# Three orders changed in a fused mixer and expert block: the second gate, the output's sum, and GpSimd's maps

## What is computed

```python
x = x + _layernorm(attn_ref(_layernorm(x)))
x = x + _layernorm(ffn_ref(_layernorm(x)))
```

```python
w = silu(einsum('btd,bthkd->bthk', h, de) * softmax(scores))
experts = einsum('bthk,bthkd->btd', w, ue)
```

## Time and profile before

| | |
|---|---|
| median of 3 runs | 2840.76 us (2839.64 to 2840.87) |
| profiled execution, its own time | 2840.37 us |
| its span, first to last instruction | 2838.7 us |
| TensorE matmuls busy | 2684.0 us, 95% |
| VectorE busy | 2449.3 us, 86% |
| GpSimd busy | 2100.9 us, 74% |
| ScalarE busy | 1737.2 us, 61% |
| mean granted clock of TensorE | 0.972 of full speed |

### The profile page before, as it was taken

The page is one execution under the profiler, slowest core; times in us unless marked ns, Lnnn a source line. Parts: engine busy times, 40 slices in busy tenths (PEclk is TensorE's granted clock), DMA queues, the critical chain, the costliest instruction groups (busy, mean ns, idle before and its releaser), DMA issues. The chain is left out here.

```text
span 2838.7 us, 50280 instructions
## 1 busy us (share of the span) xinstructions
PE 2684.0 (95%) x14720; PEld 2215.7 (78%) x14720; DVE 2449.3 (86%) x6310; ACT 1737.2 (61%) x3656; POOL 2100.9 (74%) x2689
## 2 busy tenths in 40 slices
PE   5899999999999999999999999999999999999985
PEld 4778887878887878887878887878887878887864
DVE  4588898998888998889898889988889988989985
ACT  4566666666666566666666666666666666666643
POOL 3377777877777877777877777877777877777866
PEclk9999999999999999999999999999999999999998
DMA  3000000000000000000000000000000000000000
GB/s 133 8 8 12 5 7 11 11 11 11 4 7 11 11 11 11 4 7 11 11 11 11 4 7 11 11 11 11 4 7 11 11 11 8 7 7 11 8 5 8
DMA packets 28182, 34.23 MB, mean 12 GB/s; under 512 B 2672, under 2 KB 27248, under 8 KB 27440
## 3 DMA queue, kind: packets, MB, share of 16 engines
q1 hardware_dynamic: 28144, 33.77, 3.8%
HBM read 25.37 MB, written 8.39 MB: 12 GB/s over the span
## 5 line engine op out<-in xcount | busy, mean ns | idle before, releaser
L1079 DVE SCALAR_TENSOR_TENSOR acc<-bank,cw,acc 128x253 f32<-128x253 f32 (+2 forms) x1920 | 773.5, 470 | 0.0
L1405 PE MATMUL bank<-hT,w_in 128*128 128x256 f32 x2560 | 606.3, 382 | 11.4 <-DVE acc L1079 10.8
L594 POOL TENSOR_TENSOR Em<-ee 128x1024 f32<-128x1024 f32 x256 | 578.8, 2280 | 11.3 <-issue 11.3
L1405 PEld LDWEIGHTS bank<-hT,w_in 128*128 128x128 f32 x2560 | 485.0, 192 | 118.2 <-issue 44.5
L1238 DVE SCALAR_TENSOR_TENSOR Em<-Em,p 128x1024 f32<-128x1024 f32 x256 | 407.1, 1590 | 0.0
L609 POOL TENSOR_TENSOR W<-W,Em 128x1024 f32<-128x1024 f32 x128 | 337.0, 2633 | 8.5 <-ACT Em L887 0.3
L755 ACT ACTIVATE acc<-bank,cb,cw 128x256 f32<-128x256 f32 x640 | 325.1, 561 | 0.0
L1247 DVE TENSOR_TENSOR Em<-Em,products 128x1024 f32<-128x1024 f32 x256 | 310.9, 1214 | 4.5
L887 ACT ACTIVATE Em<-Em,rden 128x1024 f32<-128x1024 f32 x256 | 292.0, 1142 | 33.9 <-DVE Em L1247 33.9
L1574 PE MATMUL products<-w_de,h2T 128*128 128x512 f32 x512 | 234.5, 601 | 17.7 <-DVE Em L1247 17.7
L736 ACT ACTIVATE xbcT<-acc 128x512 f32<-128x512 f32 x320 | 200.6, 627 | 74.1 <-DVE acc L1079 74.0
(11 more groups left out here) (196 smaller groups left out, 5578.9 us busy)
## 6 DMA issues: line engine op xcount, KB each, us to landing
x_in<-x_dram SPq DMA_DIRECT2D x32, 256.0 KB, 2.7
x_res<-x_dram SPq DMA_DIRECT2D x32, 256.0 KB, 2.7
out_dram<-f SPq DMA_DIRECT2D x32, 256.0 KB, 2.2
w_in<-in_wT_dram SPq DMA_DIRECT2D x1, 3080.0 KB, 12.0
w_up<-upT_dram SPq DMA_DIRECT2D x1, 1024.0 KB, 14.7
w_de<-down_eT_dram SPq DMA_DIRECT2D x1, 1024.0 KB, 16.7
w_down<-downT_dram SPq DMA_DIRECT2D x1, 1024.0 KB, 18.7
w_ue<-up_e_dram SPq DMA_DIRECT2D x1, 1024.0 KB, 20.8
```

Source lines behind the costliest of these rows:

```text
L594: nc.gpsimd.tensor_tensor(Em[:, k], bc(ee[:, k, 0:XD], 2, KEYS), bc(ee[:, k, XD:XD + KEYS], 1, XD), ALU.mult).then_inc(E_done.sem, 1)
L1079: ins = V.scalar_tensor_tensor(acc[:, r, a, ahead:], ps[:, a * TOK:(a + 1) * TOK - ahead], cw[:, t, k:k + 1], acc[:, r, a, ahead:], ALU.mu ...
L1405: last = mm(ring[j % 2][:, a * TOK:(a + 1) * TOK], w_in[:, k, at:at + P], hT[:, k, :], start=k == 0, stop=k == DK - 1)
```

## The change

- VectorE: the second gate and H's second step stand before the mask of head 2 of chunk 0, and `tail_sum` stands between the mask and the product of head 3.
- GpSimd: the second scaling of H stands before `ffn_root`; of chunk 1's maps only that of head 0 is formed ahead of `mixer_root_y`, and it waits for the second gate (`gate=g`); `tail_root3` follows `mixer_root_y`; the maps of heads 1, 2 and 3 stand in the next group's list, behind `tail_root4`, whose input the residual gives, and before the sums.
- ScalarE: silu of head 3's map stands in the next group's list, behind pairs 0 and 1; `ffn_norm` stands behind yT and the square of chunk 1.
- `clz` is multiplied with the divisor once for both chunks in `ffn_choose`; the product with the last expert goes into the silu as its scale, so that `ffn_last` is a copy only.
- TensorE: the product with zeros is left out; the first product of the accumulation marks the bank instead.

```diff
-            def weigh(e, c, *heads):
+            def weigh(e, c, *heads, gate=None):
+                if gate is not None:
+                    pool.wait_ge(y_done.sem, y_done.at(gate, CH - 1))
...
                 if c:
+                    weigh(f, 1, 1, 2, 3)
                     collect(f, 0, 2, 3)
...
                     mixer_scale(g, 1)
+                    mixer_decay(g, 1)
                 if c:
                     ffn_root(f)
-                if a:
-                    mixer_decay(g, 1)
-                if b:
-                    weigh(e, 1, 0, 1)
+                if b:
+                    weigh(e, 1, 0, gate=g)
                 if a:
                     mixer_root_y(g)
+                    tail_root3(g)
                 if b:
                     collect(e, 0, 1)
-                if a:
-                    tail_root3(g)
-                if b:
-                    weigh(e, 1, 2, 3)
...
-                    act.wait_ge(clz_done.sem, clz_done.at(e, c))
+                    act.wait_ge(clz_done.sem, clz_done.at(e))
+                    act.wait_ge(last_done.sem, last_done.at(e, c))
...
-                    nc.scalar.activation(cls[:], clz[:, c], ACT.Silu, accum_out=clsum[:, c:c + 1])\
+                    nc.scalar.activation(cls[:], clz[:, c], ACT.Silu, scale=last_a[:, 0:1],
+                                         accum_out=clsum[:, c:c + 1])\
...
                 pairs(0, 1)
+                if c:
+                    ffn_experts(f, 0, 3)
...
                     mixer_yT(g, 0)
-                if c:
-                    ffn_norm(f)
                 if b:
                     ffn_experts(e, 0, 1)
                 if a:
                     mixer_yT(g, 1)
                     mixer_square(g, 1)
+                if c:
+                    ffn_norm(f)
                 if b:
                     ffn_experts(e, 0, 2)
                     tail_keep(e)
-                    ffn_experts(e, 0, 3)
...
                 V.reciprocal(rden[:].rearrange("p c h -> p (c h)"), den[:]).then_inc(rden_done.sem, 1)
+                dve.wait_ge(rden_done.sem, rden_done.at(e))
+                dve.wait_ge(own_dve, own.n)
+                V.tensor_tensor(masked, masked, bc(rden[:].rearrange("p c h -> p (c h)"), 2, NC), ALU.mult)\
+                    .then_inc(clz_done.sem, 1)
...
-                dve.wait_ge(rden_done.sem, rden_done.at(e))
-                V.tensor_copy(last_a[:], fA[:, EXPERTS - 1:]).then_inc(own_dve, own.one())
-                dve.wait_ge(own_dve, own.n)
-                V.scalar_tensor_tensor(clz[:, c], clz[:, c], last_a[:, 0:1], bc(rden[:, c], 2, NC),
-                                       ALU.mult, ALU.mult).then_inc(clz_done.sem, 1)
+                if c or later(e):
+                    dve.wait_ge(cls_done.sem, cls_done.at(e, c - 1))
+                V.tensor_copy(last_a[:], fA[:, EXPERTS - 1:]).then_inc(last_done.sem, 1)
...
                     ffn_times(e, 0, 1)
-                    ffn_mask(e, 0, 2)
                 if a:
                     mixer_gate(g, 1)
                     mixer_step(g, 1)
                 if b:
+                    ffn_mask(e, 0, 2)
                     ffn_times(e, 0, 2)
                 if c:
                     ffn_store(f)
                 if b:
                     ffn_mask(e, 0, 3)
+                if a:
+                    tail_sum(g)
+                if b:
                     ffn_times(e, 0, 3)
-                if a:
-                    tail_sum(g)
...
-                    mm(f0[:], zero_b[:], mask_b[:].rearrange("p h t -> p (h t)"), start=True, stop=False)
                 for i in range(FT):
                     last = mm(f0[:, c * D:(c + 1) * D], hid[:, i, c * P:(c + 1) * P], w_down[:, i, :],
-                              start=False, stop=False)
+                              start=c == 0 and i == 0, stop=False)
```

More of the change, by code:

```diff
@@ L123, in sandwich @@
         ident_b = sb("ident_b", [P, P], BF16)
-        zero_b = sb("zero_b", [P, P], BF16)
         mask_b = sb("mask_b", [P, 4, P], BF16)
@@ L270, in sandwich @@
         Z_done = sig("Z_done", CH * RH)
-        clz_done, cls_done = sig("clz_done", CH), sig("cls_done", CH)
+        clz_done, last_done, cls_done = sig("clz_done"), sig("last_done", CH), sig("cls_done", CH)
         W_part, W_done = sig("W_part", CH * (RH - 1)), sig("W_done", CH)
@@ L341, in _ @@
             nc.gpsimd.memset(mask_b[:], 0.0).then_inc(own_pool, own.one())
-            nc.gpsimd.memset(zero_b[:], 0.0).then_inc(own_pool, own.one())
             nc.gpsimd.memset(halo[:], 0.0).then_inc(own_pool, own.one())
@@ L1325, in do_group @@
                     ffn_mask(e, 0, 3)
-                    ffn_times(e, 0, 3)
                 if a:
                     tail_sum(g)
+                if b:
+                    ffn_times(e, 0, 3)
                 dve.wait_ge(own_dve, own.n)
```

## The result

The changed kernel takes 2791.4 us (median of 4 runs, 2788.99 to 2792.48), the kernel before 2840.82 in the same comparison: a ratio of 0.9825, with an interval of 0.9808 to 0.9842. The forecast was 2746 with a range of 2718 to 2785. The gain is 49 us where 95 were forecast, and the time lies outside the range. The profiled execution took 2788.99 us.

The account below looks back on a forecast made before the run. TensorE was taken to bound the loop, at its wait for the late gate. Per group 3.1 + 0.21 - 0.2 = 3.1 us; 30 x 3.13 = 94 us off 2840.4 gave 2746, range 2718 to 2785.

Parts of the forecast that it names:

- What bounds it, and the gate: TensorE bounds the loop; its wait for the second chunk's gated y, with the low clock behind, costs 3.74 us per group.
- VectorE's walk up to the mask (1,0): Predicted times of VectorE's steps from the gate to chunk 1's head 0 mask, asked for at 1469.4.
- The new wait at `ffn_A`: TensorE's `ffn_A` for the second chunk waits for VectorE's last product, whose PSUM it overwrites: 0.65 us per group.
- rival C: The wait moves to `ffn_A`, grows to 2 us, and the clock falls there: 2830 us, chance 0.07.
- Pair 6: TensorE's pair 6 waits for VectorE's conv of pair 4, delayed by masks meeting GpSimd's work: 0.2 us more per group.
- product with zeros: Leaving out this matmul on TensorE's path saves 0.21 us per group.
- The edits of `clz`: One new VectorE multiplication in `ffn_choose`, taken as 0.35 us, hidden by 2.27 us of idle time before L1105.
- GpSimd's own lateness: GpSimd's sums for chunk 0 end 1.6 us later; its 9 us wait takes up the delay, costed at nothing.
- rival B: More port collisions, at gate or residual, or ScalarE late: 0.3 to 1 us each on `ffn_A`; 2762 to 2795, chance 0.22.
- The last groups: The groups with no mixer change little: the same maps and sums in another order.
- The best case: Neither new wait binds: 3.95 us per group, 2722 us, or 2718 if the idle time is 0.15 longer.
- The lock or a common slowing: In a VectorE and GpSimd meeting the loser stands fully; were both slowed in proportion, a group is 1 us longer, 2776 us.

Follow-up runs that it names:

- experiment 10: experiment 9 with VectorE's mask of head 2 put back in front of the second gate: 2743.07 us (one execution).
- experiment 8: The changed kernel with TensorE's product with zeros put back: 2793.04 us (one execution), period 83.81 against 83.82.
- Experiments 1: The changed kernel with `ffn_best(e, 0)` moved behind conv of pair 7 in VectorE's list: 2761.69 us.
- 2: The changed kernel with GpSimd's sums of heads 2 and 3 of chunk 1 cut to one column: 2756.5 us (one execution).
- 3: The changed kernel with GpSimd's sum of head 3 of chunk 0 cut to one column: 2741.22 us (one execution).
- experiment 11: experiment 9 plus masks of heads 2 and 3 together behind the gate, store before both products, GpSimd's map (1,0) ungated behind `mixer_root_y`: 2711.86 us.
- experiments 4: The changed kernel with `ffn_store` moved behind the last product of chunk 0 on VectorE: 2846.51 us (one execution).
- 7: The changed kernel with the last product of chunk 0 before the output's sum again on VectorE: 2826.84 us (one execution).
- experiment 9: The changed kernel with `ffn_best(e, 0)` behind conv of pair 7 and chunk 1's head 1 mask before head 0's product: 2739.36 us (one execution).

## Why the prediction was wrong

**What bounds it, and the gate: right.** The wait for y and its low clock are gone, 3.89 per group for 3.74. L1119 of the second chunk takes 0.69. Laid on the clock of the earlier trace rows (58.96 us between the two starts of S's products), VectorE's walk up to the mask (1,0) came out to a tenth or two at each step: last product at 1460.81 for 1460.7, residual at 1464.51 for 1464.5 and 1.26 long for 0.3 + 0.9, mask (1,0) at 1469.43 for 1469.4.

**The new wait at `ffn_A`: right, a little small.** 0.87 for 0.65, and the clock didn't fall (rival C). Its place and its releaser were as told. The argument against C, that the wait is too short for the clock to fall, is weaker than it looked: behind the wait of 0.67 in experiment 10 it fell three times.

**Pair 6: right in kind, mis-sized.** 0.70 for 0.2. Conv of pair 4 was over at 1489.8 (1548.75, where the next begins) for 1489.4: GpSimd's three maps began at 1468.69 for 1468.3, and the masks, 2.24 and 3.20 long, were late by as much: (1,0) ends 1.07 behind the first map, (1,1) 1.07 behind the second sum. The 0.4 is the way to `tail_root4`. It was counted from the moment when VectorE is free, 1466.7, but the mean ends at 1525.81 (1466.85) and GpSimd begins 0.27 behind that, as it did before (1470.32 to 1470.59). The step from the conv's end to pair 6 (0.13) and the 0.10 behind the gap were not counted at all. The 0.21 of the product with zeros was counted as a gain and as an earlier coming to pair 6, whose wait gives it back; it came to nothing in the sum too, and experiment 8 confirms it.

**The edits of `clz`: right.** The new multiplication (L1224) takes 0.32 for 0.35, and VectorE still sits idle for 1.90 before L1105 (2.27 before), so it is hidden.

**The step that failed** is "GpSimd's own lateness", costed at nothing. Its figures were nearly right: the sums of chunk 0 end 1.9 us later for 1.6 (1539.00, that is 1480.04, for 1478.1), and TensorE is 3 us earlier. What it asked was only whether TensorE waits for GpSimd's results, and there the 9 us wait does cover. It didn't ask which VectorE instructions the later sums would now run beside. The sums of chunk 1 stand in GpSimd's list ahead of that wait. On the clock of the earlier trace rows they end at 1500.64, 0.5 later than the 1500.11 of before, while L1175, the first instruction of `ffn_best(e, 0)` that met them, begins at 1497.68, 2.6 earlier than the 1500.32 of before. It had been only 0.2 us clear of them. It lost 2.6 us (0.60 and 2.48 for 0.21 and 0.29), conv of pair 7 came late, and pair 9 waited 0.98 per group. Experiments 1 and 2 took that wait away from both sides, and 3 showed that it and pair 6's both go with GpSimd's place. The rows for it were in the trace of before. The time lies in rival B's 2762 to 2795, but B spoke of collisions of the gate's and the residual's, each paid at `ffn_A`, and these did not come about. That B's price covers the result is luck.

**The sum.** Forecast 3.74 - 0.65 - 0.2 + 0.21 = 3.1; measured 3.89 - 0.87 - 0.70 - 0.98 + 0.21 = 1.55. Of the 1.55 between, 0.98 is pair 9, 0.50 pair 6, 0.22 `ffn_A`, and 0.15 goes the other way. The last groups, costed at no change, gave 3.6 us, and the first 2.8; why they did was not tried.

**The best case was real.** 3.95 per group with no wait at all was the bound. With the 3.89 that was measured for 3.74 it is 4.10, and experiment 11 has 4.11 and 2711.86 us, below the whole range. It took three moves in VectorE's list and one in GpSimd's, and each gave what the ledger of after had against its wait: 0.99, 0.72 and 0.89 per group.

**The lock or a common slowing.** The prediction weighed whether the loser of a meeting stands still or both run slower. Here L1179 needs 0.29 and took 2.48 beside sums that took 4.79 where they took 4.80 in the group of before, clear of it: it stood, and the sums lost nothing. The Trainium skill, page "SBUF — State Buffer", section "Who interferes with whom", says the same of the shared ports, that they are locked exclusively; the trace agrees. The error was not in this rule but in where it was applied.

What stays open: what the first and the last groups gained, and what the edits of `clz` and of ScalarE's list would do by themselves; they were not run alone.

## What to carry to other kernels

When one engine's list is moved against another's, go through both lists to the end of the period, and look at every place where an instruction of the one was just clear of a long one of the other: a margin of 0.2 us is a price that is waiting. A wait that covers an engine's lateness covers only what stands behind it, and only for those who wait by semaphore. And where several waits follow one another in a period, write them as a ledger, start to start: each of them could here be bought back for its entry to within 0.02 us, while removing 0.21 us of work ahead of a wait bought nothing. That holds where the move puts nothing else off: experiments 4 and 7 took away the wait of `ffn_A` and made the group 1.9 and 1.2 us longer.

## What the hardware showed that was not expected

- What a meeting costs goes by what is left of GpSimd's instruction and not by the size of VectorE's. Two of 32 elements, 0.29 when clear, took 2.48 us beside a sum of 2.4 (2.2 more); a mask of 1.28 took 3.20 (1.9 more).
- An instruction of VectorE that has stood gets in ahead of GpSimd's next. With two sums in a row (1554.81 to 1559.60), L1175 got through at the border of the two, near 1557.2, and L1179 then stood through the second, to 1559.64. The small run paid here for each of the two, 0.4 and 2.2. GpSimd pays too when what gets in is long: three maps with the mask (1,0) between them took 6.61 us, where one takes 1.90, and in experiment 9 two sums with the mask (1,1) between them took 5.67 for 4.78.
- The collisions that experiment 11 takes away were some 6% of VectorE's busy time: 2471.5 us in after and 2329.2 for the same instructions. Others are left: its 256 masks are busy for 408.9 us, at 1.28 each it would be 328. A busy VectorE in the page is not always a working one.
- The length of TensorE's gap alone doesn't tell whether the clock falls. Behind the 2.1 us of before it fell in each group (mean granted clock 0.972). With the 0.72 us at `ffn_A`, 0.45 at pair 6 and 0.72 at pair 9 in after it was 1.00 from 200 to 2600 us. With 0.67 us at the transposes it fell three times in the loop of experiment 10, each time for 1.7 us.
